# Second attention layer: everything that is not a score cut into pieces and spread over the five gaps of a slot

## The chip, the core and the metric

The kernel runs on one core of a Trainium2 chip. The core has a matrix engine (PE, with its weight loads PEld beside it), a vector engine (DVE), an activation engine (ACT), a general engine (POOL), and a queue processor (SP) that issues DMAs. Each runs its own instruction stream in order, and the streams meet only at semaphores. The metric is the device time of the whole program in microseconds (us).

## What is computed

Four stages follow each other on x of shape 8 x 512 x 256: an attention of another kind (layer a), a feed-forward stage with routing, the causal attention that this case is about (layer b), and the feed-forward stage again. Only layer b is touched. Cut to what matters:

```python
x = x + _L0_attn_b_ref(_layernorm(x, axis=-1), Wq, Wk, Wv, Wo)

def _L0_attn_b_ref(x, Wq, Wk, Wv, Wo):      # B 8, T 512, C 256, H 16 heads of Dh 16
    q, k, v = ((x @ W.T).reshape(B, T, H, Dh) for W in (Wq, Wk, Wv))
    q, k = _apply_rotary(q, cos, sin), _apply_rotary(k, cos, sin)
    scores = einsum('bhqd,bhkd->bhqk', q, k) * Dh ** -0.5
    attn = softmax(where(causal, -inf, scores))
    out = einsum('bhqk,bhkd->bhqd', attn, v)
    return out.reshape(B, T, C) @ Wo.T
```

## The kernel before

Layer b (`layer_b`, line 2172 on) is a software pipeline. Its step is a **slot**. The heads go through in **pairs**, 8 pairs to a batch and 64 pairs in all, and slot s works on pair s. Four pairs are a **half**, two pairs a **quad**. Every slot has five **units** u = 0 to 4 (`UNITS`), one PSUM bank each.

In each unit PE makes two things. First the turned scores of pair s (`st`, keys on the partitions, ring of banks 0 to 2), of which ACT takes the exponential (L2507) into `b_probsT`. Then the plain scores of pair s + 7 (`s`, ring of banks 3 and 4), of which DVE takes the negated row maximum (L2384, L2380). The maxima of a half are split into three bf16 parts on POOL, transposed on PE (`max`), copied by ACT and stored in DRAM (L2546), and come back as three more rows of the stacked queries (L2558, issued by `return_max` on ACT, which first waits until the store has landed). So the turned scores arrive with the maximum already taken off.

Between the score units stands all other work of PE, each item at its own slot of the batch (`FRONT`, `BACK`). Slots are counted here by s; "8n+1" is slot 1, 9, 17 and so on, where the same items stand for each batch n.

- `xT`: the normalised tokens transposed (slot 8n+3). `qk`: the four blocks of q and k (8n+4, 8n+5, 8n+8, 8n+9). `v`: two products (8n+9, 8n+10). `max`: 8n+6 and 8n+10. These are *early* items, and PE does them behind unit 1.
- `pv`: probabilities times v for a quad (bank 5). For quad m key tiles 0 and 1 are done in slot 2m+2, tiles 2 and 3 in slot 2m+3, behind unit 2.
- `o` (transpose back of `b_oT`), `attT`, `out` are *late* items behind unit 3.

The fills of xT, qk, v, max, o, attT and out take banks 6 and 7 in turn. Who empties them: ACT (`take`) the xT, v, max and attT; DVE the qk (`swap`, L2357 and L2358), o (`divide`, L2396 and L2398) and out (the addition, L2431). ACT also copies pv to `b_oT` at the end of a slot. The copy of v for batch n waits until the last pv of batch n-2 is filled, since `b_v` has two buffers.

A q or k block takes a long way: `swap` on DVE, `rotate` on POOL (L2450, L2452), `high` on ACT at unit 1 of the next slot (L2517), the rest on POOL (L2457), `middle` on ACT at unit 3 (L2522), the low part on POOL (L2459), three DMAs to DRAM (L2284) and six back into the stacks (L2289). POOL does the low part of one block before it rotates the next. The stacks made from the blocks of slots 8n+4 and 8n+5 are first read by the plain scores of slot 8n+9, those from 8n+8 and 8n+9 by slot 8n+13.

DVE takes the statistics of batch n at the start of slot 8n-15 and normalises it at the end of slot 8n-14 (`b_xn`, L2347); POOL makes the reciprocal deviation in between.

## Time and profile before

| what | value |
|---|---|
| median of 3 runs | 2420.91 us (2418.86 to 2422.22) |
| the profiled execution's own time | 2424.76 us |
| its span | 2422.5 us |
| layer b in it | about 1436 to 1988 us |
| PE busy over the span | 2175.9 us (90%) |
| DVE, ACT, POOL busy | 1457.2 (60%), 1028.3 (42%), 678.8 us (28%) |
| mean granted PE clock | 0.952 |

The span runs from the first to the last instruction of the profile; 2.3 us of the execution's own time lie outside it. In the timeline each line merges neighbouring instructions of one kind: its start, how long they took together, how many there are, and in brackets how long the engine had been idle and what ended that. In this kernel an f32 product is recorded as two instructions per call, one for each of its two passes, with the exception of the transposes. The ends of matmuls are modelled, so small idle times on PE do not all show as idle; start-to-start times do.

### The profile page before, as it was taken

The numbers are of one execution on the slowest core, as the hardware profiler recorded it, in microseconds if no ns is written. First come the engines' busy times: TensorE is split into PE (matmuls) and PEld (weight loads), VectorE is DVE, ScalarE is ACT, GpSimd is POOL, SyncE is SP. The second block draws the span as 40 slices with busy tenths as digits, with TensorE's granted clock in tenths as the row PEclk, the third lists the DMA queues.
The fourth block names the chain that finished last, engine by engine and source line by source line (L and its number), as shares of the span: only waits on it lengthen the run. The fifth ranks groups of instructions, "written<-read, shape, count | busy, mean of one in ns | idle before, by whom it ended". The sixth has DMA issues, their size and how long they took to land. (4 is left out here: it accounts for less than half of the span.)

```text
span 2422.5 us, 49703 instructions
## 1 busy us (share of the span) xinstructions
PE 2175.9 (90%) x19750; PEld 1775.6 (73%) x19750; DVE 1457.2 (60%) x3308; ACT 1028.3 (42%) x1986; POOL 678.8 (28%) x772
## 2 busy tenths in 40 slices
PE   7799999999999998798789965899999978887998
PEld 7688888888888887687589952455555547766998
DVE  2565664746566474588556645566666628874665
ACT  4343433433443343344245521455555544433554
POOL 3210110101011011266512223333333115762222
PEclk8899999999999999899899987999999999998999
DMA  7300000000000001321657755544544326113775
GB/s 237 118 19 10 10 10 10 19 2 19 10 11 10 10 2 30 104 70 53 244 180 229 221 150 101 87 75 79 84 81 81 60 76 211 44 44 114 232 225 138
DMA packets 155903, 212.71 MB, mean 88 GB/s; under 512 B 51656, under 2 KB 140000, under 8 KB 150368
## 3 DMA queue, kind: packets, MB, share of 16 engines
q1 hardware_dynamic: 142140, 191.38, 28.0%
q0 software_dynamic: 12864, 17.38, 4.3%
q8 instruction: 160, 2.62, 0.5%
q10 hardware_dynamic: 672, 0.79, 0.2%
q14 instruction: 67, 0.55, 0.1%
HBM read 141.80 MB, written 67.69 MB: 86 GB/s over the span
## 5 line engine op out<-in xcount | busy, mean ns | idle before, releaser
L2384 DVE TENSOR_REDUCE b_neg_max<-bank 128x1 f32<-128x512 f32 (+2 forms) x384 | 179.0, 507 | 141.9 <-PE bank L2617 139.8
L2507 ACT ACTIVATE b_probsT<-bank 128x512 f32<-128x512 f32 x320 | 183.1, 603 | 185.9 <-PE bank L2617 161.7
L2114 PE MATMUL bank<-e_hT_hi,k_rwkv 128*128 128x256 f32 x1088 | 214.5, 283 | 2.8 <-DVE e_hT_lo L2017 2.8
L2114 PEld LDWEIGHTS bank<-e_hT_hi,k_rwkv 128*128 128x128 f32 x1088 | 176.8, 191 | 3.6 <-DVE e_hT_lo L2017 3.6
L789 POOL TENSOR_TENSOR probs<-probs,rcp 128x512 f32<-128x512 f32 x64 | 66.8, 1044 | 345.8 <-DVE rcp L658 345.8
L2128 PE MATMUL bank<-v_rwkv_hi,e_hidden_hi 128*128 (+1 forms) x544 | 153.6, 282 | 0.0
L2128 PE MATMUL bank<-v_rwkv_hi,e_hidden_lo 128*128 (+1 forms) x544 | 153.5, 282 | 0.0
L2114 PE MATMUL bank<-e_hT_lo,k_rwkv 128*128 128x256 f32 x544 | 152.2, 280 | 0.0
L2128 PE MATMUL bank<-v_rwkv_lo,e_hidden_hi 128*128 (+1 forms) x544 | 152.1, 280 | 0.0
L2075 ACT ACTIVATE e_relu<-bank,k_bias 128x256 f32<-128x256 f32 x272 | 113.2, 468 | 73.3 <-PE bank L2114 64.5
L2617 PE MATMUL bank<-b_k_stacked,b_q_stacked 96*128 96x512 bf16 (+3 forms) x512 | 125.4, 307 | 0.0
L2617 PE MATMUL bank<-b_q_stacked,b_k_stacked 99*128 99x512 bf16 (+3 forms) x512 | 121.9, 301 | 0.0
L960 PEld LDWEIGHTS bank<-pi_t,wz 64*64 64x64 f32 x3072 | 97.2, 135 | 32.6 <-issue 23.1
L960 PE MATMUL bank<-pi_t,wz 64*64 64x64 f32 x3072 | 110.4, 221 | 3.4 <-DVE pi_t L700 3.4
L640 DVE TENSOR_TENSOR conv_lo<-bank,conv_hi 128x512 fp32r<-128x512 f32 x64 | 44.3, 692 | 109.7 <-ACT conv_hi L805 109.7
L2036 DVE TENSOR_TENSOR e_square<-e_relu 128x512 f32<-128x512 f32 x136 | 93.9, 691 | 23.4 <-ACT e_relu L2075 16.1
L2114 PEld LDWEIGHTS bank<-e_hT_lo,k_rwkv 128*128 128x128 f32 x544 | 103.7, 191 | 0.0
L2607 PE MATMUL bank<-masks,ident 128*128 128x128 bf16 x256 | 57.4, 224 | 50.9 <-DMA b_k_stacked<-scratch_b_parts 35.9
L2038 DVE TENSOR_TENSOR e_hidden_lo<-e_square,e_hidden_hi 128x512 fp32r<-128x512 f32 x136 | 94.2, 692 | 14.8 <-DVE e_square L2036 0.5
L2128 PEld LDWEIGHTS bank<-v_rwkv_hi,e_hidden_lo 128*128 128x128 f32 x544 | 102.4, 188 | 0.0
L2128 PEld LDWEIGHTS bank<-v_rwkv_lo,e_hidden_hi 128*128 128x128 f32 x544 | 102.4, 188 | 0.0
L2128 PEld LDWEIGHTS bank<-v_rwkv_hi,e_hidden_hi 128*128 128x128 f32 x544 | 102.3, 188 | 0.0
(364 smaller groups left out, 6183.1 us busy)
## 6 DMA issues: line engine op xcount, KB each, us to landing
k_rwkv<-scratch_k SPq DMA_DIRECT2D x32, 2048.0 KB, 7.4
scratch_b_parts<-b_part SPq DMA_DIRECT2D x96, 128.0 KB, 2.4
b_q_stacked<-scratch_b_parts SPq DMA_DIRECT2D x96, 128.0 KB, 4.5
b_k_stacked<-scratch_b_parts SPq DMA_DIRECT2D x96, 128.0 KB, 4.6
e_rows<-scratch_rows SPq DMA_DIRECT2D x34, 258.0 KB, 7.8
scratch_rows<-f_hq SPq DMA_DIRECT2D x16, 516.0 KB, 8.3
x_tokens<-in_x_dram SPq DMA_DIRECT2D x8, 512.0 KB, 8.1
scratch_x_out<-x_tokens SPq DMA_DIRECT2D x8, 512.0 KB, 3.7
```

Of the source, the lines that this page charges most:

```text
L640: nc.vector.tensor_tensor(lo, fills.data(*name)[:], hi.bitcast(F32), ALU.subtract).then_inc(fills.released(*name), 1)
L789: nc.gpsimd.tensor_tensor(probs, probs, spread(rcp1[:, f], NP), ALU.mult).then_inc(s["probs1_done"], 1)
L960: last = nc.tensor.matmul(data[h, j * M:(j + 1) * M], lhs[h, j], rhs[h, j], start=True, stop=True)
L2036: nc.vector.tensor_tensor(flat(sq[:, q % 2]), flat(r[:, q % 2]), flat(r[:, q % 2]), ALU.mult).then_inc(s["square_done"], 1)
L2038: nc.vector.tensor_tensor(flat(h2[1][:, q % SQ_RING]), flat(sq[:, q % 2]), flat(h2[0][:, q % SQ_RING]).bitcast(F32), ALU.subtract).then_in ...
L2075: nc.scalar.activation(r[:, q % 2, n], fl.data("h", q)[:, n * ROWS:(n + 1) * ROWS], ACT.Relu, bias=ff.k_bias[i % 2][:, 2 * c + n:2 * c + n ...
L2114: last = nc.tensor.matmul(data[:, half * ROWS:(half + 1) * ROWS], ff.k_part(i % 2, a)[:, k, at:at + P], hT[b][:, i % 2, k], start=n == 0, ...
L2128: last = nc.tensor.matmul(fl.data("e", i)[:, t * C:(t + 1) * C], h2[a][:, q % SQ_RING, half, t * P:(t + 1) * P], values[b], start=chunk == ...
L2384: last = nc.vector.tensor_reduce(neg_max[:, half % 2, t, head + e:head + e + 1], data[:, at:at + (t + 1) * P], AX_X, ALU.max, negate=True)
L2507: nc.scalar.activation(probsT[:, ring, u], fl.data("st", pair, u)[:], ACT.Exp, scale=DB ** -0.5).then_inc(fl.released("st", pair, u), 1)
L2607: nc.tensor.matmul(data[:, at:at + P], ident16[:], mask[:, 0:P], start=True, stop=False, skip_group_check=True)
L2617: last = nc.tensor.matmul(data[:, at:at + size], weights[:, tile:tile + P], moving[:, first:first + size], start=False, stop=True, skip_gr ...
```

## The change

1. The early items, the two key tiles of pv, and the late items of a slot form one list of pieces. A piece has a length of 2 (1 for key tiles 2 and 3), and qk, v and out are cut into two pieces each. The list is spread over the five gaps behind the units so that each gap gets an equal share of the length (`pieces_at`).
2. ACT's copies, the divisions, additions and swaps on DVE move with the pieces: an item whose last piece stands in gap g is taken at unit g + 1, behind that unit's exponential or maximum, and one that ends in gap 4 at unit 0 of the next slot (`made_by`). Before, ACT took the early items at unit 2 and the rest at the end of the slot, DVE swapped at unit 2 and divided and added at the end.
3. The statistics on DVE are spread over units 0 to 2 and the normalisation over units 0 to 3.
4. The loop has one slot more at its end, which holds no product.

What a slot holds, the length and order of every list of copies of ACT among themselves, POOL's and SP's instructions and all sizes stay as they were.

```diff
+MISC_PIECES = {"xT": 1, "qk": CT, "v": 2, "max": 1, "o": 1, "attT": 1, "out": 2}
...
+        def pieces_of(slot):
+
+            quad, tiles = pv_at(slot)
+            out = []
+            for name in misc_early(slot):
+                out += [(2, name, i, MISC_PIECES[name[0]]) for i in range(MISC_PIECES[name[0]])]
+            out += [(2 if kt < 2 else 1, ("pv", quad), kt, TT) for kt in tiles]
+            for name in misc_late(slot):
+                out += [(2, name, i, MISC_PIECES[name[0]]) for i in range(MISC_PIECES[name[0]])]
+            return out
+
+        def pieces_at(slot, gap):
+
+            pieces = pieces_of(slot)
+            total, so_far, out = sum(length for length, *_ in pieces), 0, []
+            for length, *piece in pieces:
+                if (2 * so_far + length) * len(UNITS) // (2 * total) == gap:
+                    out.append(piece)
+                so_far += length
+            return out
+
+        def made_by(slot, u):
+
+            at = pieces_at(slot, u - 1) if u else pieces_at(slot - 1, len(UNITS) - 1)
+            return [name for name, i, n in at if i == n - 1]
...
-                        if u == 2:
-                            for name in misc_early(slot):
-                                take(name)
+                        for name in made_by(slot, u):
+                            take(name)
...
-                        if u == 1:
-                            for name in misc_early(slot):
-                                misc(name)
-                        if u == 2 and pv_at(slot)[0] is not None:
-                            products(*pv_at(slot))
-                        if u == 3:
-                            for name in misc_late(slot):
-                                misc(name)
+                        others(slot, u)
```

On PE, slot 8n+9 (17, 25, ...) from its unit 2 on. Banks 0 to 2 are turned scores, 3 and 4 plain scores, bank 5 is pv, 6 here the q/k block, 7 here v. Before:

```order
L2645 MATMUL bank6<-b_xnT,wk_b 128x512
L2607 MATMUL bank0<-masks16,ident16 128x128 [waits bank_free0]
L2617 MATMUL bank0<-b_q_stacked0,b_k_stacked0 128x512
L2607 MATMUL bank3<-masks16,ident16 128x128 [waits bank_free3]
L2617 MATMUL bank3<-b_k_stacked2,b_q_stacked2 128x512
L2675 MATMUL bank5<-b_probsT,b_v 32x256 x4
L2675 MATMUL bank5<-b_probsT,b_v 32x128 x4
L2611 MATMUL bank1<-masks16,ident16 128x256 [waits bank_free1]
```

The same slot of the change, from unit 3 on:

```order
L2634 MATMUL bank1<-masks16,ident16 128x256 [waits bank_free1]
L2640 MATMUL bank1<-b_q_stacked0,b_k_stacked0 128x384
L2640 MATMUL bank1<-b_q_stacked0,b_k_stacked0 128x128
L2634 MATMUL bank4<-masks16,ident16 128x2x128 [waits bank_free4]
L2640 MATMUL bank4<-b_k_stacked2,b_q_stacked2 128x384
L2640 MATMUL bank4<-b_k_stacked2,b_q_stacked2 128x128
L2669 MATMUL bank6<-b_xnT,wk_b 128x512
L2626 MATMUL bank2<-masks16,ident16 128x2x128 [waits bank_free2]
L2640 MATMUL bank2<-b_q_stacked0,b_k_stacked0 128x256 x2
L2626 MATMUL bank3<-masks16,ident16 128x2x128 [waits bank_free3]
L2640 MATMUL bank3<-b_k_stacked2,b_q_stacked2 128x256 x2
L2699 MATMUL bank5<-b_probsT,b_v 32x256 x4
```

The last key tiles of the quad stood behind unit 2, ahead of units 3 and 4; now they stand behind unit 4, at the very end of the slot.

On ACT, slot 8n+10 (18, 26, ...) from its unit 1 on; `b_oT` in the row ahead of it is the copy of pv. Before:

```order
L2517 ACTIVATE b_part0<-b_rotated 128x512 [waits b_parts_stored,b_rot_done]
L2507 ACTIVATE b_probsT<-bank2 128x512 [waits bank_full2,bank_full5]
L2536 ACTIVATE b_v<-bank7 128x16x16 [waits bank_full5,bank_full7]
L2536 ACTIVATE b_v<-bank7 128x16x16
L2544 ACTIVATE b_max_rows<-bank6 24x512 [waits bank_full6,b_max_stored]
L2546 DMA scratch_b_max<-b_max_rows 24x512 [waits bank_free6]
L2507 ACTIVATE b_probsT<-bank0 128x512 [waits bank_full0,bank_full5]
L2522 ACTIVATE b_part1<-b_rotated 128x512 [waits b_rest_done]
L2507 ACTIVATE b_probsT<-bank1 128x512 [waits bank_full1,bank_full5]
L2507 ACTIVATE b_probsT<-bank2 128x512 [waits bank_full2,bank_full5]
L2558 DMA b_q_stacked1<-scratch_b_max 3x4096 [waits b_max_stored,bank_full0]
```

The change:

```order
L2544 ACTIVATE b_part0<-b_rotated 128x512 [waits b_parts_stored,b_rot_done]
L2534 ACTIVATE b_probsT<-bank2 128x512 [waits bank_full2,bank_full5]
L2563 ACTIVATE b_v<-bank7 128x16x16 [waits bank_full5,bank_full7]
L2563 ACTIVATE b_v<-bank7 128x16x16
L2534 ACTIVATE b_probsT<-bank0 128x512 [waits bank_full0,bank_full5]
L2571 ACTIVATE b_max_rows<-bank6 24x512 [waits bank_full6,b_max_stored]
L2573 DMA scratch_b_max<-b_max_rows 24x512 [waits bank_free6]
L2549 ACTIVATE b_part1<-b_rotated 128x512 [waits b_rest_done]
L2534 ACTIVATE b_probsT<-bank1 128x512 [waits bank_full1,bank_full5]
L2534 ACTIVATE b_probsT<-bank2 128x512 [waits bank_full2,bank_full5]
L2589 DMA b_q_stacked1<-scratch_b_max 3x4096 [waits b_max_stored,bank_full0]
```

One exponential has moved ahead of the copy and the store of the maxima; the fetch that waits for the store stands where it stood, behind the first exponential of slot 8n+11.

## Rows read from the trace of the kernel before

**Rows 1.** By stretch: span, PE, PEld, DVE, ACT, POOL, clock, DMA share, GB/s.

```profile
1540.00:1900.00 360.00, 334.66 (x2524) 194.63 (x2520) 231.08 (x529) 191.73 (x371) 134.98 (x167) 0.99 0.48 82
...
1714.27:1738.83 24.56, 22.91 (x176) 13.96 (x175) 14.31 (x32) 13.65 (x28) 8.51 (x7) 1.00 0.60 100
1738.83:1765.09 26.26, 25.41 (x199) 14.00 (x197) 18.44 (x40) 14.48 (x28) 9.52 (x13) 1.00 0.54 93
```

**Rows 2.** Waits of PE, 1512 to 1968: total us, times, longest.

```profile
PE bank L2607 <- DMA b_k_stacked<-scratch_b_parts: 13.1, 8, 4.7
PE bank L2641 <- DVE b_xn L2347: 6.9, 6, 1.3
```

**Rows 3.** Timeline of PE, slot 25 and the first products of slots 27 and 28.

```profile
1707.00 0.23 PE L2607 MATMUL bank<-masks,ident 128*128 128x128 bf16 x1 [0.58 <-DMA b_k_stacked<-scratch_b_parts]
...
1709.73 1.88 PE L2645 MATMUL bank<-b_xnT,wk_b 128*128 128x512 f32 x4
...
1711.78 0.38 PE L2617 MATMUL bank<-b_k_stacked,b_q_stacked 96*128 96x512 bf16 x1
1712.09 0.86 PE L2675 MATMUL bank<-b_probsT,b_v 128*32 128x256 f32 x16
1712.88 0.28 PE L2611 MATMUL bank<-masks,ident 128*128 128x256 bf16 x1
...
1722.11 0.38 PE L2617 MATMUL bank<-b_q_stacked,b_k_stacked 99*128 99x512 bf16 x1
...
1729.60 0.38 PE L2617 MATMUL bank<-b_q_stacked,b_k_stacked 99*128 99x512 bf16 x1
```

**Rows 4.** Timeline of PE, all of layer b: waits for the k stack, and two others.

```profile
1584.56 0.23 PE L2607 MATMUL bank<-masks,ident 128*128 128x128 bf16 x1 [1.46 <-DMA b_k_stacked<-scratch_b_parts]
...
1645.85 0.23 PE L2607 MATMUL bank<-masks,ident 128*128 128x128 bf16 x1 [2.96 <-DMA b_k_stacked<-scratch_b_parts]
...
1646.80 3.63 PE L2650 MATMUL bank<-wv_b,b_xnT 128*128 128x256 f32 x8
...
1707.94 1.94 PE L2650 MATMUL bank<-wv_b,b_xnT 128*128 128x256 f32 x8
...
1766.08 0.23 PE L2607 MATMUL bank<-masks,ident 128*128 128x128 bf16 x1 [0.61 <-DMA b_k_stacked<-scratch_b_parts]
...
1826.62 0.23 PE L2607 MATMUL bank<-masks,ident 128*128 128x128 bf16 x1 [1.98 <-DMA b_k_stacked<-scratch_b_parts]
...
1968.71 1.71 PE L2675 MATMUL bank<-b_probsT,b_v 128*32 128x512 f32 x16 [1.33 <-ACT b_oT L2500]
```

**Rows 5.** Busy time by stretch around the wait at 1645.85; columns as in Rows 1.

```profile
1645.00:1650.00 5.00, 4.15 (x16) 3.22 (x17) 2.25 (x9) 1.11 (x2) 2.54 (x4) 0.69 0.02 3
```

**Rows 6.** Timeline of POOL, slots 26 and 30: low parts and the rotation between.

```profile
1714.81 1.16 POOL L2459 TENSOR_TENSOR b_part<-b_rotated,b_part 128x512 bf16<-128x512 f32 x1 [2.77 <-ACT b_part L2522]
1715.92 1.27 POOL L2450 TENSOR_TENSOR b_swapped<-b_swapped,sin 128x512 f32<-128x512 f32 x1
...
1752.48 1.16 POOL L2459 TENSOR_TENSOR b_part<-b_rotated,b_part 128x512 bf16<-128x512 f32 x1 [1.34 <-ACT b_part L2522]
```

**Rows 7.** Timeline of ACT, slots 18, 19, 25 to 27 and 51.

```profile
1661.25 0.30 ACTq L2546 DMA_DIRECT2D scratch_b_max<-b_max_rows  x1
...
1666.57 1.09 ACT L2507 ACTIVATE b_probsT<-bank 128x512 f32<-128x512 f32 x2 [2.84 <-DMA scratch_b_max<-b_max_rows]
...
1713.07 0.66 ACT L2536 ACTIVATE b_v<-bank 128x256 f32<-128x256 f32 x2 [0.50 <-PE bank L2675]
...
1718.57 0.63 ACT L2517 ACTIVATE b_part<-b_rotated 128x512 bf16<-128x512 f32 x1 [1.88 <-POOL b_rotated L2452]
...
1720.71 0.33 ACTq L2546 DMA_DIRECT2D scratch_b_max<-b_max_rows  x1
...
1722.67 0.24 ACTq L2558 DMA_DIRECT2D b_q_stacked<-scratch_b_max  x1
...
1905.43 1.58 ACT L2507 ACTIVATE b_probsT<-bank 128x512 f32<-128x512 f32 x3 [2.04 <-DMA scratch_b_max<-b_max_rows]
```

More of the change, by code:

```diff
@@ L2413, in _ @@
                         fill_ones()
-                    if batch_at(slot, FRONT["stats"]) is not None:
-                        statistics(batch_at(slot, FRONT["stats"]))
                     for u in range(len(UNITS)):
@@ L2418, in _ @@
                             maximum(scored(slot), u)
[L2419 to L2421 removed]
+                        for name in made_by(slot, u):
+                            if name[0] == "qk":
+                                if name[1:] == (0, 0):
                                     ready((s["loaded"], LOADS))
[L2423 to L2431 removed]
+                                swap(*name[1:])
+                            if name[0] == "o":
+                                divide(name[1])
+                            if name[0] == "out":
+                                add_out(*name[1:])
+                        if batch_at(slot, FRONT["stats"]) is not None:
+                            statistics(batch_at(slot, FRONT["stats"]), u)
+                        if batch_at(slot, FRONT["xn"]) is not None and u < TT:
+                            normalise(batch_at(slot, FRONT["xn"]), u)
             @block.gpsimd
@@ L2550, in take @@
                         copy(attT[:, name[2]], name)
+                    if kind == "pv":
+                        if n:
+                            act.wait_ge(*full("o", n - 1))
+                        copy(oT[:], name)
                 def return_max(n, f):
@@ L2573, in _ @@
                                 high(n, step)
-                        if u == 2:
-                            for name in misc_early(slot):
-                                take(name)
+                        for name in made_by(slot, u):
+                            take(name)
                         if u == 3:
@@ L2579, in _ @@
                                 middle(n, step)
-                    quad, tiles = pv_at(slot)
-                    if 3 in tiles:
-                        if quad:
-                            act.wait_ge(*full("o", quad - 1))
-                        copy(oT[:], ("pv", quad))
-                    for name in misc_late(slot):
-                        take(name)
             @block.tensor
@@ L2659, in misc, with products @@
                             last = nc.tensor.transpose(data[:, t * P:(t + 1) * P], oT[:, t * P:(t + 1) * P], core.ident[:])
-                    last.then_inc(fl.filled(*name), 1)
-                def products(quad, tiles):
+                    if i == pieces - 1:
+                        last.then_inc(fl.filled(*name), 1)
+                def products(quad, kt):
                     n, q = divmod(quad, NQUADS)
-                    if 0 in tiles:
+                    if kt == 0:
                         for k in range(CT):
@@ L2669, in products, with others @@
                     data = fl.data("pv", quad)
-                    for kt in tiles:
-                        size = T - kt * P
-                        for i in range(QUAD):
-                            pair, e = quad * 2 + i // 2, i % 2
-                            u, at = {0: (2 * e, 0), 1: (2 * e + 1, P), 2: (4, 2 * P * e), 3: (2 * e + 1, 0)}[kt]
-                            last = nc.tensor.matmul(data[i * 32:(i + 1) * 32, kt * P:], v[:, n % 2, kt, q * QUAD + i, :],
-                                                    probsT[:, pair % PROBS_RING, u, at:at + size], start=kt == 0, stop=kt == TT - 1,
-                                                    skip_group_check=True)
-                    if TT - 1 in tiles:
-                        last.then_inc(fl.filled("pv", quad), 1)
+                    size = T - kt * P
+                    for i in range(QUAD):
+                        pair, e = quad * 2 + i // 2, i % 2
+                        u, at = {0: (2 * e, 0), 1: (2 * e + 1, P), 2: (last_unit, 2 * P * e), 3: (2 * e + 1, 0)}[kt]
+                        last = nc.tensor.matmul(data[i * 32:(i + 1) * 32, kt * P:], v[:, n % 2, kt, q * QUAD + i, :],
+                                                probsT[:, pair % PROBS_RING, u, at:at + size], start=kt == 0, stop=kt == TT - 1,
+                                                skip_group_check=True)
+                    if kt == TT - 1:
+                        last.then_inc(fl.filled("pv", quad), 1)
+                def others(slot, gap):
+                    for name, i, pieces in pieces_at(slot, gap):
+                        if name[0] == "pv":
+                            products(name[1], i)
+                        else:
+                            misc(name, i, pieces)
                 pe.wait_ge(s["loaded"], LOADS)
```

105 lines of the change are left out of this document (48 added, 57 removed).

## The prediction

> **What bounds the kernel now.** I read the busy times by stretch first. In the long steady part of layer b PE is busy for 334.7 of 360 us, DVE for 231, ACT for 192, all at a clock of 0.99 [rows 1]. So PE's stream is the bound there, and the change can win only what PE loses between its products, 7% of layer b.
>
> The waits of PE name two large losses [rows 2]: 13.1 us in which the plain scores wait for the k stack to come back from DRAM, and 6.9 us in which `xT` waits for the normalisation on DVE. Then I followed eight slots in the timeline. The plain scores of slot 25 begin at 1707.00 [rows 3], slots 26 to 28 last from 1714.27 to 1738.83, slots 29 to 32 to 1765.09 [rows 1], and the plain scores of slot 33 begin at 1766.08 [rows 4]. So the period of about 59 to 61 us has two parts with different limits. From slot 25 to slot 29 PE is limited by itself and by who empties its banks. From slot 29 to slot 33 it is limited by one chain: a k block is multiplied in slot 29, is swapped, rotated and split, its low part ends at 1752.48 + 1.16 = 1753.64 [rows 6], is stored and loaded back by nine DMAs, and PE is let go at 1766.08 [rows 4]. That is 27.25 us from the start of slot 29, and PE had 0.6 us of idle time in hand.
>
> **Price of the cut itself.** The pv products use 32 columns of the array each, all others 128 or 24. Ahead of pv the last score product (512 columns) takes 0.31 us start to start where 512 columns at 2.4 GHz are 0.21, so 0.10 us is paid on entry. The block of key tiles 2 and 3 takes 0.79 us to the next mask [rows 3]; two passes of 256 + 128 columns, at the rate of v (8 x 256 columns from 1707.94 to 1709.73 [rows 3, 4]), are 0.67, so 0.12 is paid on leaving it. Each pv block that is split pays 0.2 us more, between 0.1 (if only one side counts) and 0.25. By the list of pieces, 51 of the 62 blocks in slots 2 to 63 are split: 10 us, not in one sum but slot by slot below.
> By the Trainium skill, "TensorEngine Tiling (Array Packing)", Key Properties, a change of the tiling mode drains the array; this speaks against the change and agrees with the two 0.1 us of the rows, and if it cost nothing the sum below would come out 10 us lower at most. The other items have the mode of the scores, and splitting them I cost at nothing: 512 f32 columns follow each other alike whatever stands ahead.
>
> **Slots 29 to 32 and their like (six times).** Now the k block of slot 29 ends in gap 2 instead of gap 1. Its swap waits for the maximum of unit 3, and ends about 6.3 us into the slot. But what had held the rotation was not the swap: POOL first does the low part of the q block, which needs ACT's `middle` at unit 3, and unit 3 came behind 1.7 us of q/k product and a pv block. With one half block ahead of it, unit 3 is at 3.8 us, `middle` at 4.4, the low part over at 6.3. The rotation begins at 6.4 instead of 7.8. Everything behind it (`high`, the max copy, now one unit earlier, `middle` of slot 30, low part, stores, loads) moves by 1.4 to 1.5 us, so the k stack is there after 25.8 instead of 27.25 us. PE itself takes 26.26 us for the four slots now, 25.41 of them busy [rows 1]. By start-to-start times more is lost than the 0.85 idle, since a modelled end covers part of a wait: 2.0 us (an estimate: 0.6 for a bank in slot 29, 0.3 for maxima in slot 30, 1.1 for exponentials in slot 31). Spreading removes these waits, and 4 x 0.2 us come on for pv: 25.1, and 25.4 to the plain scores. The chain still ends last, with a DMA wait as before. Gain 1.45 us, six times: **-8.7**.
>
> **Slots 25 to 28 and their like (five times).** Here the change adds two waits on ACT. First: the copy of v waits for the last pv of batch n-2. That pv stood behind unit 2, and the wait was 0.50 us [rows 7]; now it stands in gap 4, and ACT, at unit 2, waits to the end of the slot, with `exp(3)`, `middle`, `exp(4)` queued behind. Count from 1707.00. The slot's PE work, the same as before, takes 7.2 us (to 1714.27), and pv is full at its end: 7.15, v is copied from 7.35, `middle` runs at 8.35, where it ran at 7.1 (v at 1713.07 [rows 7], one exponential and 1.0 us later). POOL's low part moves from 7.81 to 9.07, and the first rotation to 10.2; `high` follows 2.65 us behind that start (1715.92 to 1718.57 [rows 6, 7]), so at 12.8 instead of 11.6. PE loses 0.35 us in slot 26 for the bank of v. Second: behind `high` the max rows are stored at 13.7 (1720.71 [rows 7]); now one exponential more stands ahead: 12.8 + 0.54 (`high`) + 0.48 (exponential) + 0.54 (v) + 0.48 (exponential) + 0.6 (max copy) = 15.4, each the start-to-start time of such an instruction behind 1718.57, that is 0.4 us into slot 27 rather than 1.4 us ahead of it. ACT fetches the rows at unit 0 of slot 27 and stands still until the store has landed: 1661.25 to 1666.2, 5.0 us, in batch n=2; only 1720.71 to 1722.67, 2.0 us or less, where no stack loads were in flight [rows 7]. With 4.9 us ACT resumes 5.7 us into slot 27 where it resumed at 3.9 before.
> Who waits: `attT` takes bank 6, which holds xT until ACT has copied it (exponential, copy: 6.85 us), and PE is there at 4.8: 2.0 us lost. The q block of slot 28 waits 0.9 us for the copy of attT, `out` 0.25 for the swap, the second xT 0.6 for the division. Against that the wait for the normalisation (1.15 to 1.3 us [rows 2]) and 0.3 + 0.3 + 0.5 us of small waits go. Slot 26 stays at 7.84 us, slot 27 goes from 7.5 to 8.35, slot 28 from 9.2 to 10.1 (they began at 1714.27, 1722.11 and 1729.60, slot 29 at 1738.83 [rows 1, 3]): +1.7. With 3.5 us to landing it is about zero, with 2.0 us -1.1 (slot 27 then takes 6.4). The landing depends on how far SP's loads of the q stack have got, 2.75 to 4.7 us behind its stores. I take three long, one in between (+0.8) and one short (-0.4): **+5.5**.
> The k stack of slot 29 comes 1.3 us later as well, but was 1.7 to 4.6 us early: nothing.
>
> **Slots 49 to 66.** In slot 51 the same stall of ACT (2.04 us [rows 7]) meets no xT, but the turned scores of unit 4 wait for it, and in slot 52 pv in gap 0 for the exponential just ahead: slots 51 and 52 +2.6. Slots 53, 55, 56 lose their waits for DVE (-2.2), the others -0.6 net of the cuts, and the wait of 1.33 us for `b_oT` at 1968.71 [rows 4] goes, since pv of quad 30 now ends in gap 1: **-1.5**.
>
> **Slots -7 to 4.** No exponentials here. The k block of slot -7 is swapped at unit 0 of slot -6, 1.6 us later, which shows at slot -3 but goes into the 4.7 us wait of slot 1 [rows 2]. That wait hangs on slots -4 and -3, whose swaps move by 0.4 and about 1.3 us, and on SP, which was busy with the q loads meanwhile: +0.2. The k block of slot 1 is swapped in slot 2, +1.3 at slot 5; the wait for xT in slot 3 is lost in that. **+1.5**.
>
> **The clock.** After 2.96 us idle at 1645.85 the granted clock was 0.69 for 5 us [rows 4, 5], which is the level of 1.2 GHz for part of it, and v took 3.63 instead of 1.94 us [rows 4]: 1.7 us. At 1826.62 (1.98 us idle) the clock fell too, at 1584.56 (1.46) not. The new wait of 2.0 us, of which some 1.85 would show as idle, lies between. I give it one or two falls in the five: **+2**. The extra slot holds no instruction that waits: 0. So is the spread of statistics: POOL's deviation comes at 6 us into slot 25 instead of 4, ahead of `middle` at 8.35.
>
> **Sum.** -8.7 + 5.5 - 1.5 + 1.5 + 2 = -1.2 us. Against the profiled execution's own 2424.8 that is 2423.6. That execution was 3.9 above the median of the runs, so the forecast stands at 2420.9 - 1.2 = 2419.7 us.
>
> **The rivals.** Within 0.2% (4.8 us) is about what a measurement of this kernel can tell from no change.
> - *About no change (the forecast), 0.42.* The three gains and losses around 6 to 9 us nearly cancel. Its own range: splits at 0.1 or 0.25 us (-2, +1), landings one class better or worse (-3, +2), so 2414 to 2425.
> - *Faster, 0.30.* The max rows land in 2 to 3 us, since their store has moved against the q loads, so ACT never holds PE: slots 25 to 28 give 5 x -1.1, slots 51 and 52 nothing, no clock falls. -8.7 - 5.5 - 4.1 + 1.5 = -16.8: 2404. For it speaks the row at 1722.67, against it four of five batches with 3.5 to 5.4 us.
> - *Slower, 0.20.* The wait at `attT` turns the clock down: it decides from an idle time that lies between 1.46 and 1.98 us. Then each of the five batches and slot 51 pay 1.7 us: 6 x 1.7 in place of 2, and with it the landings are all long (1.7 x 5 in place of 5.5): +10: 2431.
> - *The chain does not get shorter, 0.08.* The stores and loads take from 12.2 to 14.7 us behind the low part already. If they only wait elsewhere, the -8.7 is gone: +7.5: 2428.
>
> **Numbers.** The range has to reach into the cases of both signs, since each holds 2 in 10 or more: from 2405, where the faster case is nearly whole, to 2432. Faster takes its case and the lower end of the forecast's: 0.33; slower 0.20 + 0.06: 0.26; the same 0.41.
>
> **What the profile after would show.** Waits of PE for `b_xn` gone (6.9 us); `b_v` waiting for pv some 3 us six times; ACT behind the store of the max rows 3 us and more; new waits of PE for `b_xnT` or the bank behind it near 2 us per batch; from slot 29 to slot 33 25.8 us; pv blocks in two. I would be wrong if PE does not wait at `attT`, or if the time from slot 29 to slot 33 stays at 27 us.

## The result, and the profile after

The changed kernel takes 2425.5 us (median of 17 runs, 2420.7 to 2428.9), the kernel before on the same chips 2419.8 (17 runs, 2413.4 to 2422.5). The ratio is 1.0029, with a 95% interval of 1.0022 to 1.0036: the change is slower, by some 7 us. That is 0.3%. The forecast was 2419.7, 1.2 us less than before, with "slower" as the least likely side.

The profiled execution after took 2427.5 us. Busy time by stretch, the columns as in [rows 1]; the second stretch is slots 26 to 28, the third slots 29 to 32:

```profile
1540.00:1900.00 360.00, 336.01 (x2519) 188.53 (x2518) 239.08 (x527) 194.56 (x373) 136.43 (x167) 1.00 0.47 82
1712.12:1737.97 25.85, 23.32 (x177) 13.73 (x176) 16.35 (x34) 15.31 (x31) 8.92 (x8) 1.00 0.56 95
1737.97:1763.63 25.66, 25.52 (x199) 13.61 (x197) 18.23 (x40) 14.75 (x27) 9.85 (x14) 1.00 0.55 95
```

Counted from their first products on PE, slots 26 to 28 went from 24.56 to 25.85 us and slots 29 to 32 from 26.26 to 25.66, and PE has almost no idle time left in the latter (25.52 of 25.66 busy). The waits of PE from 1512 to 1984 (total us, times, longest):

```profile
PE bank L2630 <- DMA b_q_stacked<-scratch_b_max: 9.4, 6, 3.4
PE bank L2666 <- ACT b_xnT L2527: 6.9, 5, 2.5
PE bank L2630 <- DMA b_k_stacked<-scratch_b_parts: 3.3, 6, 1.1
```

Of the two losses that [rows 2] named, the one for `b_xn` has fallen to 0.2 us and the one for the k stack from 13.1 to 3.3 us (with the wait at slot -3, which lies ahead of this window, from 15.0 to 9.3). PE's waits for the maxima of DVE fell as well, from 6.2 to 0.8 us. In their place PE waits 9.4 us for the returned maximum (3.4 before; 3.4 of the 9.4 in slot 0) and 6.9 us at `attT`, whose bank still holds xT.

From here on a slot begins with its first exponential on ACT, unless PE is named; on PE, which runs ahead, the same loss can show a slot later. Where the time went, from starts in the timelines (before, after): first scores to slot 5, 84.1 and 86.4 us; slots 5 to 48, 330.7 and 325.3; slot 49 to the last exponential, 80.4 and 84.6; from there to the last product, 12.2 and 13.5. So the steady part gained 5.4 us, and both ends lost. The start lost more than it seems, since the 84.1 hold one slot of 15.1 us (slot 1) that takes 8.5 to 9.3 in most other traces. In the start the row that stands out is PE's wait before the plain scores of slot -3, 5.98 us after where it was 1.89:

```profile
1502.12 0.29 PE L2630 MATMUL bank<-masks,ident 128*128 128x128 bf16 x1 [5.98 <-DMA b_k_stacked<-scratch_b_parts]
```

and on POOL, in slot -7, what stands ahead of that stack. After the change:

```profile
1478.59 0.23 POOL L2470 TENSOR_SCALAR b_var<-b_mv 128x4 f32<-128x4 f32 x1 [15.42 <-DVE b_mv L2364]
1478.90 1.04 POOL L2472 TENSOR_TENSOR b_rstd<-b_var,neg_half 128x4 f32<-128x4 f32 x1
1479.91 1.16 POOL L2484 TENSOR_TENSOR b_rotated<-b_rotated,b_part 128x512 f32<-128x512 f32 x1
```

Before:

```profile
1463.37 0.23 POOL L2443 TENSOR_SCALAR b_var<-b_mv 128x4 f32<-128x4 f32 x1
1463.68 1.04 POOL L2445 TENSOR_TENSOR b_rstd<-b_var,neg_half 128x4 f32<-128x4 f32 x1
1464.69 1.15 POOL L2457 TENSOR_TENSOR b_rotated<-b_rotated,b_part 128x512 f32<-128x512 f32 x1
```

The aggregates that `b_var` needs now stand on DVE behind the maximum of unit 2, and that maximum waits for scores that wait for the stacks. POOL sat 15.4 us in front of its deviation, with the rest of a q block queued behind it. How much of PE's wait hangs on this, e1 tells: little.

### The profile page after: what moved, and what is told of

It is laid out like the page before. It is cut to its first block and busy times, and to the rows that moved or that the text cites. A ratio compares the mean times of both kernels' runs of the same rounds, so it can differ in the third digit from the quotient of the medians.

```text
span 2425.3 us, 49703 instructions
## 1 busy us (share of the span) xinstructions
PE 2178.6 (90%) x19750; PEld 1767.6 (73%) x19750; DVE 1470.1 (61%) x3308; ACT 1032.8 (43%) x1986; POOL 680.5 (28%) x772
## 3 DMA queue, kind: packets, MB, share of 16 engines
q1 hardware_dynamic: 142140, 191.38, 27.8%
## 5 line engine op out<-in xcount | busy, mean ns | idle before, releaser
L2534 ACT ACTIVATE b_probsT<-bank 128x512 f32<-128x512 f32 x320 | 187.0, 601 | 155.3 <-PE bank L2640 124.7
L2053 POOL DMA_INDIRECT scratch_x_out<-e_y,e_token x34 | 53.7, 1578 | 163.3 <-DVE e_y L2025 158.2
```

The lines of the kernel that those rows point to most:

```text
L2053: nc.gpsimd.indirect_dma_start(x_out[:, :], bass.IndirectOffsetOnAxis(token[:, i % 3, t:t + 1], 0), y[:, i % 2, t, :], None, compute_op=AL ...
L2534: nc.scalar.activation(probsT[:, ring, u], fl.data("st", pair, u)[:], ACT.Exp, scale=DB ** -0.5).then_inc(fl.released("st", pair, u), 1)
```

## The experiments

All times are medians; the kernel before had 2418.0 to 2419.8 in the four sets of runs, so small differences between kernels of different sets are better read from the ratios. Single runs of one kernel spread over 5 to 15 us, so a profile shows a mechanism and the median its price. Two figures show how far one trace can be off: the first deviation of layer b, ahead of all that the edits touch, comes between 1428.96 and 1435.37 us, and e7, e11 and e12, whose programs are the same below slot 2, take 44.2, 44.6 and 48.0 us from the first scores to slot 0.

| run | us | ratio to before, 95% interval |
|---|---|---|
| changed kernel | 2425.5 | 1.0029 [1.0022, 1.0036] |
| e1: + statistics first, batches 0, 1 | 2424.3 | 1.0022 [1.0008, 1.0035] |
| e5: + statistics first, all | 2425.8 | 1.0028 [1.0018, 1.0038] |
| e3: + pv ahead of v | 2425.8 | 1.0026 [1.0015, 1.0038] |
| e9: e5 and e3 together | 2410.6 | 0.9973 [0.9960, 0.9987] |
| e7: e9 and old places below slot 2 | 2410.9 | 0.9967 [0.9955, 0.9979] |
| e6: e1 and old places below slot 2 | 2428.8 | 1.0044 [1.0029, 1.0059] |
| e4: + PE's old order | 2447.1 | 1.0119 [1.0096, 1.0142] |
| e14: e4 + statistics first | 2424.0 | 1.0032 [1.0019, 1.0044] |
| e13: before + statistics spread | 2449.0 | 1.0129 [1.0112, 1.0147] |
| e8: before + normalisation spread | 2416.5 | 0.9995 [0.9984, 1.0006] |
| e2: changed, pv blocks whole | 2436.5 | 1.0068 [1.0048, 1.0088] |
| e11: e7, pv blocks whole | 2418.7 | 0.9999 [0.9985, 1.0014] |
| e10: changed, q loads after the maximum | 2435.6 | 1.0071 [1.0054, 1.0089] |
| e12: e7, k block in gap 0 | 2413.6 | 0.9982 [0.9968, 0.9995] |
| e15: e9, maximum ahead of v | 2411.5 | 0.9968 [0.9956, 0.9979] |

**One part undone at a time.** e1 puts the statistics of the first two batches back at the slot's start:

```diff
+                    n = batch_at(slot, FRONT["stats"])
+                    if n is not None and n < 2:
+                        for u in range(len(UNITS)):
+                            statistics(n, u)
                     for u in range(len(UNITS)):
...
-                        if batch_at(slot, FRONT["stats"]) is not None:
-                            statistics(batch_at(slot, FRONT["stats"]), u)
+                        if n is not None and not (n < 2):
+                            statistics(n, u)
```

> The statistics and aggregates of batches 0 and 1 (slot -7 for batch 1) stand at the slot's start again, the rest is the changed kernel. Theory A (the start lost time because the aggregates of slot -7 queue behind the maxima, whose scores wait for the stacks; the deviation then holds POOL): the deviation starts at about 1463.5 instead of 1478.6, the wait for the k stack at slot -3 (5 to 6 us in the changed kernel) falls to about 2, the layer begins its full slots 3 to 5 us earlier: 3 to 5 us faster than the changed kernel. Theory B (the k block of slot -7 that moved behind slot -7's own gaps is what delays the stacks): the deviation moves but the wait of slot -3 stays over 4 us, and the time stays within 1.5 us of the changed kernel.

In its trace the start is 4.6 us shorter (81.8 us from the first scores to slot 5, 86.4 in the changed kernel), but the median moved by 1.2 us only, which these runs can't tell from nothing. The deviation of slot -7 now comes at 1460.88 without a wait, and yet PE waits at slot -3:

```profile
1497.11 0.29 PE L2634 MATMUL bank<-masks,ident 128*128 128x128 bf16 x1 [5.08 <-DMA b_k_stacked<-scratch_b_parts]
```

These are the signs of theory B, which blames the place of the k block of slot -7. In all traces with the changed gaps in the start this wait is 4.9 to 7.3 us, and 1.5 to 3.2 us in all those with the old ones, wherever the statistics stand. What the spread statistics cost there is some 3 us of the stretch ahead of slot -3: 29.0 to 29.9 us with them, 26.0 to 26.6 without, at the changed gaps. e2 keeps each pv block in one gap:

```diff
+                at = (2 * so_far + length) * len(UNITS) // (2 * total)
+                if piece[0][0] == "pv":
+                    at = block if piece[1] % 2 else at
+                    block = at
```

> The two key tiles of a pv block stand in one gap again, everything else is spread as in the changed kernel. Theory A (each cut of a pv block costs about 0.2 us of TensorE at entry and exit, 51 of them): about 8 to 10 us faster than the changed kernel, less what the coarser gaps give back, so 5 to 10 us faster. Rival (the cuts lie in waits or cost under 0.05 us): within 2 us of the changed kernel.

It is 11 us slower. Slots 13 to 16 do get 1.0 us shorter (24.55 against 25.54), so the cuts do cost what the prediction said, some 0.25 us each. But what PE no longer spends there it waits elsewhere. Two rows of e2, slots 17 and 41:

```profile
1649.09 0.23 PE L2634 MATMUL bank<-masks,ident 128*128 128x128 bf16 x1 [3.48 <-DMA b_k_stacked<-scratch_b_parts]
...
1840.42 0.23 PE L2634 MATMUL bank<-masks,ident 128*128 128x128 bf16 x1 [3.64 <-DMA b_k_stacked<-scratch_b_parts]
```

After each, the clock falls (0.66 in the 5 us behind 1840), and these slots last 14.5 and 14.7 us instead of 9.9 and 9.6. That is 9.7 us; more is lost in slots 8n+2 to 8n+4, 135.2 us in the five batches instead of 123.6, where PE's waits at `attT` rise from 6.9 to 10.8 us and five waits for the swap, 5.0 us together, are new. This trace is of the slowest of e2's six runs (2444.2), so it shows more loss than the median has. e3 lists the pv pieces ahead of the early ones in slots 8n+1:

```diff
-                out += [(2, name, i, MISC_PIECES[name[0]]) for i in range(MISC_PIECES[name[0]])]
+                early += [(2, name, i, MISC_PIECES[name[0]]) for i in range(MISC_PIECES[name[0]])]
             out += [(2 if kt < 2 else 1, ("pv", quad), kt, TT) for kt in tiles]
+            out = out + early if early and early[0][1][0] == "v" and early[0][1][2] == 0 else early + out
```

> In the slots in which the first half of v of a batch is made (8n+1), the pv pieces come ahead of the early pieces, so ScalarE's copy of v no longer stands behind the pv block of its own slot. Theory A (ScalarE held at that wait, 3.6 us each, makes the cast of the high part, and with it the chain of the maximum, late): ScalarE's wait of v for PE falls from 21 us in 6 to under 5 in all, slots 8n+2 to 8n+4 get 0.5 to 1 us shorter each time: 2 to 5 us faster than the changed kernel. Rival (the length of these slots is set by the store of the maximum and its landing, that stays as it is): within 1.5 us.

ACT's 21.3 us in six waits of v for pv are gone, and nothing is won: the rival's outcome. Another wait of ACT has come, of `middle` for POOL's rest, which the changed kernel's trace doesn't have in its steady part (waits of ACT, 1560 to 1990), and `high` waits 17.3 us for the rotation where it waited 11.8:

```profile
ACT b_part L2550 <- POOL b_rotated L2485: 9.1, 5, 1.9
```

e4 gives PE its old order and leaves the rest spread (the place of a piece is `2 if kind == "pv" else 3 if kind in ("o", "attT", "out") else 1`):

> TensorE's order is that of the kernel before (early products in gap 1, pv in gap 2, late in gap 3, uncut), the statistics, the normalisation and the takers stay spread as in the changed kernel. Theory A (slots 8n+2 to 8n+4 and the last slots lose by the order on TensorE, the start by the statistics): slots 8n+2 to 8n+4 return to about 24.5 us from 26.5, the k-stack chain returns to about 27.5 us, the start stays late: 2417 to 2422 on the scale of the kernel before at 2419.8, so 3 to 7 us faster than the changed kernel. Rival (the spread DVE work is what lengthens those slots): slots 8n+2 to 8n+4 stay at 26 us or more and the time is that of the changed kernel or longer.

Theory A was wrong, and the rival came true beyond its words: on PE slots 8n+2 to 8n+4 take 26.6 to 29.4 us, and the time is 22 us over the changed kernel's. Something that the change spreads is bad for the old order.

**Pairs.** e5 is e1 for all batches; e6 is e1 with all products of slots below 2 in gap 1; e7 is e5 and e3 with that same start; e8 is the kernel before with `normalise(n, u)` behind unit u.

> The changed kernel with the statistics and aggregates of every batch at the start of their slot again (slots 8n+1). Theory A (the spread aggregates hold GpSimd's deviation by 3.7 us in each batch, GpSimd's rotation of the next k block comes 1.6 us late and ScalarE waits for it): the deviation starts 3 us earlier, ScalarE's wait for b_rotated from GpSimd falls from 11.8 us in 6, the slots 8n+1 to 8n+4 get 0.5 to 1.5 us shorter each batch: 3 to 8 us faster than the run that undid it in the first two batches alone (2424.3), so 2416 to 2421. Rival (2.4 us of statistics ahead of the first maxima delay the scores of slot 8n+1 by as much as the late deviation costs): 2423 to 2427.

> The changed kernel with the start of the layer as in the kernel before: the products of slots below 2 all in gap 1 and uncut by gaps, and the statistics of batches 0 and 1 at the slot's start. Theory A (the start costs the changed kernel 6 us, of which the statistics are about 2 and the placement of the k blocks of slots -11 and -7 the rest): from the first scores to slot 0 about 40 us as in the kernel before, against 44.3 with the statistics alone undone: 3 to 5 us faster than that run, 2419 to 2422. Rival (the start is given back at slot 1, which waits in both kernels for the stacks of the second half): within 1.5 us of 2424.3.

> Three edits together on the changed kernel: statistics at the slot's start in every batch, the products of slots below 2 in gap 1 again, and the pv pieces ahead of v in slots 8n+1. If the gains add (start 4 to 6, statistics 3 to 5, pv ahead of v 1 to 3): 2410 to 2417, faster than both kernels. If the chain of the k stack and the store and return of the maximum set the batch whatever TensorE's order is, what is won ahead of them turns into waits for DMA b_k_stacked and b_q_stacked: 2418 to 2423.

> The kernel before with one part of the change alone: the four normalisations of a batch stand one in each of the first four units of their slot. Theory A: TensorE's wait for b_xn (6.9 us in 6 waits before) falls under 1 us and the time goes with it: 2413 to 2416. Rival (the time goes into the next wait for the returned maximum): within 1.5 us of the kernel before, with the waits for b_q_stacked longer by what the waits for b_xn lost.

e5 wins nothing (ACT's wait of v for pv, 21.3 us, is still there), and e6 seems to lose, yet all three together win 15 us and beat both kernels. e8 takes away all of the 6.9 us for `b_xn` and moves the median by less than the runs can tell: PE now waits 3.1 us at `attT` for `b_xnT`, 1.2 more for the maxima and 0.9 more for the returned ones. e9, without e7's start, then told which pair it was:

> Two of the three edits of the fast run (2410.9) on the changed kernel: statistics at the slot's start in every batch, and pv ahead of v in slots 8n+1; the start is left as changed. Theory A (the low part of the q block of slot 8n waits for both GpSimd's rest, behind the deviation, and ScalarE's cast of the middle part, behind the copy of v; one edit alone leaves the other wait, both together bring the stores of the parts 2 to 3 us forward): stores of the q parts at 7.5 to 8.5 us into slot 8n+1 as in the fast run (10.4 to 11.7 in the changed kernel), landing of the maximum about 3 us after its issue, the five steady batches as short as in the fast run; 2411 to 2416. Rival (the products of slots below 2 in one gap are what won): 2422 to 2427.

It is the pair. The join is the low part of the q block made in slot 8n, which POOL finishes in slot 8n+1. It needs ACT's `middle`, which stands on ACT behind the copy of v, which waits for the last pv; and `middle` needs POOL's rest, which stands behind the deviation, which waits for the aggregates. ACT in slot 9, changed kernel:

```profile
1592.21 0.66 ACT L2563 ACTIVATE b_v<-bank 128x256 f32<-128x256 f32 x2 [3.30 <-PE bank L2699]
1592.76 0.60 ACT L2534 ACTIVATE b_probsT<-bank 128x512 f32<-128x512 f32 x1
1593.24 0.64 ACT L2549 ACTIVATE b_part<-b_rotated 128x512 bf16<-128x512 f32 x1
```

POOL there:

```profile
1589.96 0.23 POOL L2470 TENSOR_SCALAR b_var<-b_mv 128x4 f32<-128x4 f32 x1 [3.70 <-issue]
1590.28 1.04 POOL L2472 TENSOR_TENSOR b_rstd<-b_var,neg_half 128x4 f32<-128x4 f32 x1
1591.29 1.17 POOL L2484 TENSOR_TENSOR b_rotated<-b_rotated,b_part 128x512 f32<-128x512 f32 x1
1593.95 1.23 POOL L2486 TENSOR_TENSOR b_part<-b_rotated,b_part 128x512 bf16<-128x512 f32 x1 [1.50 <-ACT b_part L2549]
```

The rest ends at 1592.46, the copy of v lets `middle` go at 1593.24: each wait hides most of the other. That is why one alone wins nothing. The pair costs 13.5 us by the ratios to the kernel before, 14.9 by the medians; in the two traces slots 8n+2 to 8n+4 go from 132.1 to 124.7 us on PE in five batches. With both gone (e9, slot 9 from 1576.61) the low part starts 7.0 us into the slot instead of 9.6, and SP's queue reads, first the changed kernel, slot 9 from 1584.36:

```profile
1595.21 1.31 SPq L2306 DMA_DIRECT2D scratch_b_parts<-b_part  x3
1597.97 2.69 SPq L2311 DMA_DIRECT2D b_q_stacked<-scratch_b_parts  x6
1602.66 1.31 SPq L2306 DMA_DIRECT2D scratch_b_parts<-b_part  x3
1606.07 2.72 SPq L2311 DMA_DIRECT2D b_k_stacked<-scratch_b_parts  x6
```

then e9:

```profile
1584.80 1.34 SPq L2307 DMA_DIRECT2D scratch_b_parts<-b_part  x3
1587.57 2.69 SPq L2312 DMA_DIRECT2D b_q_stacked<-scratch_b_parts  x6
```

The stores stand 8.2 us into the slot instead of 10.9. In the changed kernel the maximum is stored just as the last of the six loads is issued, and ACT, which wants it back, stands for 3.26 us:

```profile
1600.42 0.30 ACTq L2573 DMA_DIRECT2D scratch_b_max<-b_max_rows  x1
...
1605.29 0.24 ACTq L2589 DMA_DIRECT2D b_q_stacked<-scratch_b_max  x1
1605.63 0.60 ACT L2534 ACTIVATE b_probsT<-bank 128x512 f32<-128x512 f32 x1 [3.26 <-DMA scratch_b_max<-b_max_rows]
```

In e9 the loads have been out for 2.25 us by then:

```profile
1592.51 0.29 ACTq L2578 DMA_DIRECT2D scratch_b_max<-b_max_rows  x1
...
1595.31 0.24 ACTq L2594 DMA_DIRECT2D b_q_stacked<-scratch_b_max  x1
1595.65 0.60 ACT L2539 ACTIVATE b_probsT<-bank 128x512 f32<-128x512 f32 x1 [1.20 <-DMA scratch_b_max<-b_max_rows]
```

The fetch comes 2.8 us behind the store instead of 4.9. Over the six slots 8n+2 from slot 10 on it comes 2.6 to 4.7 us behind, 3.7 to 5.6 in the changed kernel. The copies of xT on ACT come earlier, and PE's waits for `b_xnT` and, from slot 1 on, for the returned maximum fall from 6.9 + 6.0 to 2.3 + 3.9 us.

**Is it the loads that hold the store?** e10 makes SP wait for the stored maximum ahead of those six loads:

```diff
                     sp.wait_ge(s["parts_stored"], (at - 1) * 48)
+                    if n and step == 2:
+                        sp.wait_ge(s["max_stored"], 16 * 2 * n)
```

> The changed kernel, in which SyncE issues the six loads of the q stack of the second half only when the stored maximum of the half before has landed. Theory A (the store of the maximum takes 3.7 to 5.7 us to land because it stands behind those six loads in the DMA queues, and ScalarE, which waits for it, holds the copies of xT and so TensorE at attT): landing in 2 to 2.5 us, TensorE's waits for b_xnT (6.9 us) and for the returned maximum (9.4 us) fall to half or less, slots 8n+3 and 8n+4 1 to 2 us shorter: 5 to 9 us faster than the changed kernel, 2416 to 2421. Rival (the landing doesn't depend on the loads, or the k stack that follows them becomes late): landing still over 3.5 us, or waits for b_k_stacked longer by 5 us and more in all; 2424 to 2432.

ACT in slots 10 and 11, with the queues empty:

```profile
1598.63 0.30 ACTq L2575 DMA_DIRECT2D scratch_b_max<-b_max_rows  x1
...
1600.03 0.25 ACTq L2591 DMA_DIRECT2D b_q_stacked<-scratch_b_max  x1
```

and SP:

```profile
1600.08 3.06 SPq L2313 DMA_DIRECT2D b_q_stacked<-scratch_b_parts  x6
1603.18 1.41 SPq L2306 DMA_DIRECT2D scratch_b_parts<-b_part  x3
1608.91 2.69 SPq L2313 DMA_DIRECT2D b_k_stacked<-scratch_b_parts  x6
```

Here, and in four of the other five slots 8n+2, the landing took 1.4 to 1.5 us at most (3.2 in one), and slot 11 fell from 7.7 to 5.2 us: that half of the theory held. But now the stores of the k parts stand behind the q loads and need 5.7 us from their issue to the k loads (3.4 in the changed kernel), so the k stack is late and PE waits 27.8 us for it from 1512 on instead of 3.3. The rival's half set the time: 10 us slower.

**Further edits of e7** (the expectations' "fast run")**.** e11 repeats e2's edit on e7, e12 puts the k blocks of side 1 whole into gap 0 of their slots.

> The fast run (2410.9, three edits undone) with the two key tiles of each pv block in one gap again. On the changed kernel the same edit cost 11 us. Theory A (the whole blocks do save about 1 us of TensorE in the slots 8n+5 to 8n+8, and it turned into waits for the k stack, because its chain was already the bound): here, with a chain that has 2 us more room, slots 8n+5 to 8n+8 are 24.5 us instead of 25.5 and the waits for the k stack grow by less than they save: 2405 to 2412. Rival (whole blocks crowd gap 2 of slots 8n+2 and 8n+4, where the exponentials and the maxima then wait, whatever the chain): slots 8n+3 and 8n+4 longer by 1 us and more, 2413 to 2422.

> The fast run (2410.9) with the k block of slots 8n+5 (and the one of slot -3 and below) whole in gap 0 instead of cut between gaps 0 and 2. Theory A (that block heads the chain of the k stack, 25.5 to 26 us long against as much work of TensorE): the k stack comes 1.5 to 2.5 us earlier, TensorE's wait for it at slots 8n+1 (3.8 us in 6) falls under 1: 2407 to 2411. Rival (the wait is already covered, and two more products in gap 0 delay the scores there): 2411 to 2415.

Against e7's trace, e11 saves 0.8 and 1.0 us in slots 13 to 16 and 37 to 40 and nothing in slots 21 to 24 and 29 to 32, loses 0.6 in each slot 8n+4 (10.4 against 9.8), and its median is 8 us over e7's; slot 41 alone took 12.9 us in its trace. Nothing speaks for whole blocks, and why the median is so much higher its one profile shows only in part. e12 doesn't win: slots 8n+5 get 0.6 us longer.

**Which spread part hurts the old order.** e13 is the kernel before with the statistics spread as in the change, e14 is e4 with e5's edit.

> The kernel before with one part of the change alone: the statistics two each behind the maxima of units 0 and 1, the aggregates behind those of unit 2. Theory A (the spread statistics are what the change loses by: in the old gaps the maxima of unit 2 come behind the products of gap 1, so the aggregates and GpSimd's deviation come 4 to 6 us later, its rest stands behind them, and ScalarE's cast of the middle part, ahead of its exponentials, waits for the rest): the cast of the middle part about 2.5 us later in each slot 8n+1, a slower start of the layer as well: 2430 to 2442. Rival (the late deviation is covered by the copy of v and the cast's own place at unit 3): 2416 to 2421.

> The run with TensorE's old order and everything else spread (2447.1), now with the statistics and aggregates at the slot's start. Theory A (its 28 us over the kernel before are the late deviation): slots 8n+1, 12 us there, fall to 9 to 10 where the k stack is in time, and the time to 2415 to 2423. Rival (the copy of pv, which stands ahead of the cast of the middle part on ScalarE there, or the takers spread over the units, are what is slow with that order): 2430 and more.

e13 alone costs 31 us, somewhat more than e4 over the kernel before, and e14 gives some 21 of e4's 27 back (by the ratios). The 6 to 8 us that e14 still has over the kernel before must lie in the other parts that it spreads; e8 found the normalisation free, and the new places of the copies, swaps and divisions were not run by themselves. POOL and ACT of e13 in slot 9:

```profile
1597.10 0.23 POOL L2445 TENSOR_SCALAR b_var<-b_mv 128x4 f32<-128x4 f32 x1 [5.21 <-issue]
...
1598.42 1.16 POOL L2459 TENSOR_TENSOR b_rotated<-b_rotated,b_part 128x512 f32<-128x512 f32 x1
```

```profile
1595.62 0.66 ACT L2538 ACTIVATE b_v<-bank 128x256 f32<-128x256 f32 x2 [0.20 <-PE bank L2677]
1596.16 0.60 ACT L2509 ACTIVATE b_probsT<-bank 128x512 f32<-128x512 f32 x1
1599.61 0.63 ACT L2524 ACTIVATE b_part<-b_rotated 128x512 bf16<-128x512 f32 x1 [2.84 <-POOL b_rotated L2459]
```

In the old order 3.8 us of v and k products stand in gap 1, between the maxima of units 1 and 2, and the aggregates stand behind them. ACT, with the last exponentials queued behind `middle`, waits 2.8 us for POOL; slots 8n+1 last 11.4 to 12.5 us. e6 had the same flaw in slot 1, whose statistics it left spread over a slot with all products in gap 1 (POOL waited 4.27 us there, slot 1 took 12.2 us).

**The place of the maximum.** e15 is e9 with `("max", n, f)` first in its slot:

> The run with two edits undone (2410.6), with the transposes of the maximum ahead of v in slots 8n+2 and of xT and qk in the others. Theory A (the maximum is stored 1.5 us earlier, the queues being empty by then, and comes back as much earlier; TensorE's waits for it, 3.9 us in 3, and for b_xnT, 2.3, go): 2406 to 2409. Rival (the store now meets the last loads of the q stack and takes 4 us and more to land, or the transposes in gap 0 wait for GpSimd's split): 2410 to 2415.

The store went out at 1592.66 in slot 10, while SP issued the q loads from 1589.20 to 1592.86, and the fetch came 4.35 us later (3.9 to 5.0 in the six such slots, 2.6 to 4.7 in e9): the earlier store went into a longer landing, as the rival said.

## Why the prediction was wrong

The waits that the prediction named all came: v for pv 21.3 us in six, ACT behind the store up to 4.0 us, PE at `attT`. What failed is how they were priced.

- **The spread of statistics (priced at 0) beside the late v (priced inside +5.5).** This is the step whose mechanism failed. "POOL's deviation comes at 6 us into slot 25 instead of 4, ahead of `middle` at 8.35" was right as a reading (5.6 us into slot 9), and the price of 0 holds as long as v is late: e5 has the changed kernel's time. But the cover that it named was a `middle` that the change itself had made late. The two waits were each other's cover. Together they cost some 14 us (e9 against the changed kernel), each alone nothing (e5 and e3, +0.3), and the sum has no place for such a pair. The slots that carry the pair's cost are the next term and the one for slots 49 to 66. In slot -7 there was no such cover at all, and I had not asked there what the maxima wait for.
- **Slots 25 to 28 (+5.5).** The mechanism was right: v waits for pv (3.6 us at most), the store is late, ACT stands, PE waits at `attT` 1.4 to 2.5 us in three batches and in the others for the returned rows. Over the five batches the three slots 8n+2 to 8n+4 cost +9.2 on PE instead of +5.5. That the landing hangs on the q loads is shown by e10 and supported by e9 and e15; the classes of landing were a guess, and the real ones were 3.7 to 5.6 us.
- **Slots 29 to 32 (-8.7).** Near in sum: 10.5 us less over six batches from slot 8n+5 to the plain scores of slot 8n+9. But the batch that the sum was worked out on, slots 29 to 33, gave 0.6 us and not 1.45; the others gave 3.0, 3.0, 1.7, 2.4 and -0.3, most where the kernel before had its long waits for the k stack. The agreement is in part luck.
- **Price of the cut (10 us in the sums).** Confirmed in size by e2, 1.0 us in four slots with four cut blocks. But removing it made both kernels slower (e2, e11), so these 10 us could not be had by leaving the blocks whole.
- **Slots 49 to 66 (-1.5).** The most mis-sized term: the trace shows +4.2 to the last exponential and +1.3 behind it. Slots 49 and 52 took 1.8 and 3.0 us more, 60 and 62, where pv stands in gap 0, 1.8 and 0.6, and two falls of the clock came on, one behind the row below, one in the last output products (5.38 us for 16 where e7 has 3.69). What the prediction priced there came: slots 51 and 52 +2.9 for +2.6, slots 53, 55 and 56 -2.4 for -2.2. It had nothing for slot 49, where the late v holds ACT as well, nor for 60 and 62. With v no longer late (e3) slots 49 to 52 take 30.4 us, against 33.8 in the changed kernel and 28.7 before. The fall in the output products comes in four of the 17 traces and hangs on no one edit.

```profile
1907.64 0.28 PE L2626 MATMUL bank<-masks,ident 128*128 128x256 bf16 x1 [2.26 <-ACT b_probsT L2534]
```

- **Slots -7 to 4 (+1.5).** +2.3 against the profiled execution of before, about +6 against the 80.3 us that this stretch took in e8, which has the old start but for the normalisation. Traces of one and the same start differ by up to 4 us, so this term is not settled.
- **The clock (+2).** No fall in slots 5 to 48, where before had two. The falls of before came behind its waits of 2.96 and 1.98 us for the k stack, and went with them: -3.1 us in five slots 8n+1, from their plain scores to the next slot on PE, a gain that the sum left out. That the new wait at `attT` brought none was not foreseen and may be luck: the "slower" rival has the clock decide from an idle time between 1.46 and 1.98 us, and the changed kernel idles for 2.49 us at 1787.51 with a granted clock of 1.00 in the 5 us behind it.
- **The reference.** The sum was made on an execution of 2424.8 us, 5 us above the median of before in the later runs. Part of that excess is the one long slot 1 (15.1 us, 8.5 in e8 with the same program there). So the difference of the two profiled executions (+2.7) is smaller than that of the medians (+5.7 to +7).

In short: without the pair of waits the change is worth -6.5 us (e9), with it +7. Even -6.5 is well short of the -16.8 that the prediction gave its "faster" rival, in which ACT never holds PE: in e9 the store still takes up to 4.7 us to land.

## What to carry to other kernels

When a change makes two inputs of one instruction later, price each with the other removed: the cover that makes one free may be the other. Before moving statistics behind work of the same engine, follow who reads them and what stands behind that reader in its own queue. Where a chain through DRAM bounds a stage, faster products turn into waits, and the clock can fall behind such a wait on top (3.48 and 3.64 us in e2).

## What the runs showed of the hardware

- How fast a small store (24 KB) lands depends on the traffic ahead of it. The fetch behind it was issued 1.4 to 1.5 us later in six of seven stores of e10 that no load stood close ahead of (3.2 in the seventh), 2.6 to 3.7 us later in four stores of e9 behind six loads of 128 KB whose issue had ended 2.2 to 2.3 us earlier, and 4.5 to 5.6 us later in the four of the changed kernel that were issued together with the last of the six. The stores of the k parts went from 3.4 to 5.7 us in the same way (e10). The store is issued by ACT and the loads by SP, so the two queues don't shield each other. This agrees with the Trainium skill, "DMA: Bandwidth & Descriptors", Issuing engines are not separate DMA queues, and with its section Queues, rings and completion order, by which a DMA's semaphore write comes only behind every earlier write of the same DMA engine, across its queues; no run here tells the two apart.
- PE's granted clock fell after idle times of 1.98 us (before, 1826.62), 2.26 (changed kernel, 1907.64), 3.48 and 3.64 us (e2), but also after 1.76 us (e5, 1573.4) and 1.23 us (e11, 1568.4). It was 0.66 to 0.68 in the 5 us behind each, so the level of 1.2 GHz for part of them. It did not fall after 1.46 us [rows 4], nor after 2.10 us (e6, 1612.0) or 2.49 us (changed kernel, 1787.5), where it was 1.00. So in these traces the length of the one idle time doesn't tell whether the clock falls.
- Mode changes to the 32-column products cost 0.25 us per extra block where nothing else was in the way (e2, slots 13 to 16), in line with the 0.1 us for each direction read in [rows 3]. This agrees with the Trainium skill, "TensorEngine Tiling (Array Packing)", Key Properties, which says that such a change drains the array, without a figure.
